# A three-layer expert FFN: its third layer as Strassen products over expert sums, with operands streamed from DRAM

## What is computed

```python
def _L0_ffn_ref(x, Wr, br, W1, b1, g1, be1, m1, v1, W2, b2, g2, be2, m2, v2, Wo, bo):
    feat = jnp.mean(x, axis=0)
    w = jax.nn.softmax(feat @ Wr + br, axis=-1)
    h = jnp.einsum('bfd,edh->bfeh', x, W1) + b1
    h = jax.nn.relu(_bn(h, g1, be1, m1, v1))
    h = jnp.einsum('bfeh,ehk->bfek', h, W2) + b2
    h = jax.nn.relu(_bn(h, g2, be2, m2, v2))
    y = jnp.einsum('bfeh,ehd->bfed', h, Wo) + bo
    return jnp.einsum('bfed,fe->bfd', y, w)

x = x + _L0_gnn_ref(_layernorm(x, axis=-1), adj, L0_gnn_W, L0_gnn_a)
x = x + _L0_ffn_ref(_layernorm(x, axis=-1), ...)
```

## Time and profile before

| | |
|---|---|
| median of 3 runs | 2948.12 us |
| the profiled execution: its own time, its span | 2946.45 us, 2944.7 us |
| mean granted TensorE clock | 0.994 |
| busy: PE, PEld | 2884.2 us (98%), 2423.9 us (82%) |
| busy: DVE, ACT, POOL | 1931.2 us (66%), 1697.9 us (58%), 730.2 us (25%) |
| DMA | 145.60 MB, mean 49 GB/s; 14 to 23 GB/s in the second stage |

### The profile page before, as it was taken

How to read it: one execution, slowest core, us unless ns; L and a number is a source line. 1 busy time by engine, 2 the same in 40 slices (tenths; PEclk the granted TensorE clock), 3 DMA queues, 4 the chain that set the end, 5 groups by cost and what they waited for, 6 DMA issues and landing times.

```text
span 2944.7 us, 42543 instructions
## 1 busy us (share of the span) xinstructions
PE 2884.2 (98%) x14806; PEld 2423.9 (82%) x14806; DVE 1931.2 (66%) x2843; ACT 1697.9 (58%) x2620; POOL 730.2 (25%) x894
## 2 busy tenths in 40 slices
PE   7999999998999999999999999999999999999998
PEld 7989898998888888888888888888888888888887
DVE  7999999996555555655556565556555565655554
ACT  7889888987444545444444445454544444454544
POOL 5888888887100000000000000000000000000000
PEclk9999999999999999999999999999999999999999
DMA  4444444443100000000000000000000000000000
GB/s 153 150 155 155 150 156 152 156 141 111 57 15 14 21 21 14 14 14 14 14 14 14 14 14 14 14 14 14 23 20 14 14 14 14 14 14 14 14 15 15
DMA packets 86037, 145.60 MB, mean 49 GB/s; under 512 B 7744, under 2 KB 63464, under 8 KB 86000
## 3 DMA queue, kind: packets, MB, share of 16 engines
q1 hardware_dynamic: 86000, 145.13, 14.7%
HBM read 111.52 MB, written 33.59 MB: 49 GB/s over the span
## 4 chain that ended last, share of the span: by engine, by line
PE 75%; DVE 0%; ACT 0%; issue 0%
PE z_ps L54 16%; PE z_ps L52 16%; PE z_ps L53 16%; PE y_ps L54 8%; PE y_ps L53 8%; PE y_ps L52 8%; PE turn_ps L931 1%; PE turn_ps L941 1%; PE y_ps L1016 0%; PE turn_ps L965 0%; PE y_ps L965 0%; PE z_ps L1009 0%; PE y_ps L1009 0%; ACT h L1048 0%; DVE h L1140 0%; DVE h_lo L1146 0%
## 5 line engine op out<-in xcount | busy, mean ns | idle before, releaser
L1048 ACT ACTIVATE h<-z_ps,bn_shift,bn_scale 128x512 f32<-128x512 f32 x1024 | 741.8, 775 | 1077.5 <-PE z_ps L54 1075.9
L1127 DVE TENSOR_TENSOR h_lo<-h,h_hi 128x1024 fp32r<-128x1024 f32 x256 | 321.6, 1256 | 762.5 <-ACT h_hi L1065 762.5
L86 POOL TENSOR_TENSOR ffn_vareps<-ffn_mv,ln_eps 128x4 f32<-128x4 f32 x32 | 6.4, 201 | 1880.0 <-DVE ffn_mv L80 1880.0
L52 PE MATMUL z_ps<-h_hi,w_hi 128*128 128x512 f32 x1024 | 410.3, 401 | 0.0
L54 PE MATMUL y_ps<-h_hi,wo_lo 128*128 128x512 f32 x1024 | 406.8, 397 | 0.0
L1140 DVE TENSOR_TENSOR h<-h,w_bc 128x1024 f32<-128x1024 f32 x256 | 313.8, 1226 | 140.9 <-ACT h L1048 137.0
L54 PE MATMUL z_ps<-h_hi,w_lo 128*128 128x512 f32 x1024 | 405.8, 396 | 0.0
L52 PE MATMUL z_ps<-xT_hi,w_hi 128*128 128x512 f32 x1024 | 405.2, 396 | 0.0
L53 PE MATMUL z_ps<-xT_lo,w_hi 128*128 128x512 f32 x1024 | 405.1, 396 | 0.0
L54 PE MATMUL z_ps<-xT_hi,w_lo 128*128 128x512 f32 x1024 | 405.0, 396 | 0.0
L53 PE MATMUL z_ps<-h_lo,w_hi 128*128 128x512 f32 x1024 | 405.0, 395 | 0.0
(11 more groups left out here) (128 smaller groups left out, 4876.6 us busy)
## 6 DMA issues: line engine op xcount, KB each, us to landing
adj_sb<-in_adj SPq DMA_DIRECT2D x128, 512.0 KB, 3.4
x_sb<-in_x SPq DMA_DIRECT2D x64, 256.0 KB, 2.8
x_scratch<-x_sb SPq DMA_DIRECT2D x128, 128.0 KB, 1.8
ffn_x<-x_scratch SPq DMA_DIRECT2D x32, 512.0 KB, 3.3
out<-ffn_x SPq DMA_DIRECT2D x32, 512.0 KB, 2.9
w_stage<-in_L_ffn_W SPq DMA_DIRECT2D x16, 256.0 KB, 4.0
w_bc<-w_scratch SPq DMA_DIRECT2D x8, 512.0 KB, 7.3
w_bc<-in_L_ffn_Wo SPq DMA_DIRECT2D x4, 512.0 KB, 5.9
```

What stands on the lines that cost most here:

```text
L52: pe.matmul(out, w_hi, x_hi, start=first, stop=False)
L86: pool.tensor_tensor(self.vareps[:, :], self.mv[:, :, 1], self.ln_eps[:, :], ALU.add) \
L1048: return act.activation(dst[:, m, :], src[:, m, :], ACT.Relu, bias=bn_shift[layer][:, col], scale=bn_scale[layer][:, col])
L1127: dve.tensor_tensor(h1_lo[i][:, :, :], h1[:, :, :], bits(h1_hi[i][:, :, :]), ALU.subtract) \
```

## The change

It touches `ffn_block` alone, in four ways.

First, layer three is a 2 x 2 block product, (2 x 128 outputs) x (2 x 128 inputs) on (2 x 256 nodes), done with Strassen's seven products in Winograd's form instead of eight. Each product has 256 columns and three split terms, 21 matmuls for a step. The seven products add up over the 8 experts in seven half banks (`m_ps`, 4 banks), and are combined once a tile.

Second, both sides of the products need sums. For the activations VectorE forms four differences from the gated h2 in each step (T1 and T3 in one instruction, then T2, then T4, each from the one before); h2's upper parts, now 7 x 256 = 1792 columns, are rounded by ScalarE in two copies, the lower ones subtracted by VectorE in two pieces. For Wo, GpSimd, ScalarE and VectorE form seven operands for each expert during the first tile and SyncE stores them to DRAM (`wo_dram`); from the second tile on they are loaded back step by step into two buffers (896 KB each), and a gate row too (256 KB, `load_gate`). The seven products of a tile are copied out by ScalarE and combined by seven adds on GpSimd (`combine`); for the last tile VectorE does this.

Third, `m_ps` needs four banks and `turn_ps` gets one, so layers one and two share three: `z1_bank, z2_bank = (0, 1), (2, 0)`. Bank 0 is used by both, and each half of a layer has its own semaphore count. Layer one now runs four steps ahead. TensorE's slot is layer two, transposes, layer three, layer one; the transposes come in groups of four in four slots.

Fourth, `residual` writes to buffers of its own (`res`), so x is loaded earlier, and xT is double buffered.

The core of the diff ("..." for what is left out):

```diff
+    Z1, Z2, Y = 4, 2, 1
+    PRODUCTS = ((P1, A11, B11), (P2, A12, B21), (P5, S1, T1), (P7, S3, T3), (P6, S2, T2), (P3, S4, B22), (P4, A22, T4))
...
-        z1_ps, z2_ps, y_ps, turn_ps = ps("z1_ps"), ps("z2_ps"), ps("y_ps"), ps("turn_ps")
+        z_ps, m_ps, turn_ps = ps("z_ps", 3), ps("m_ps", 4), ps("turn_ps", 1)
+        z1_bank, z2_bank = (0, 1), (2, 0)
...
+            def combine(n):
+                done = (n - 1) * COMBINES
+                pool.wait_ge(S["prod_ready"], n)
+                wait(pool, S["out_psum"], 2 * (n - 1))
+                def put(dst, left, right, op):
+                    pool.tensor_tensor(dst, left, right, op).then_inc(S["comb_ready"], 1)
+                put(prod[:, P6, :], prod[:, P1, :], prod[:, P6, :], ALU.add)
+                put(yT_sb[:, 0, HALF:], prod[:, P1, :], prod[:, P2, :], ALU.add)
+                pool.wait_ge(S["comb_ready"], done + 1)
+                put(prod[:, P7, :], prod[:, P7, :], prod[:, P6, :], ALU.add)
+                put(yT_sb[:, 0, :HALF], prod[:, P5, :], prod[:, P6, :], ALU.add)
...
+            def y_layer(e, w, x_hi, x_lo):
+                for q, a, t in PRODUCTS:
+                    w_hi, w_lo, x = w[:, 0, a - 1, :], w[:, 1, a - 1, :], t - 1
+                    begins = e == 0 and q in (P1, P2, P5, P4)
+                    pe.matmul(m_at(q), w_hi, x_hi[:, x, :], start=begins, stop=False, skip_group_check=True)
+                    pe.matmul(m_at(q), w_hi, x_lo[:, x, :], start=False, stop=False, skip_group_check=True)
+                    done = pe.matmul(m_at(q), w_lo, x_hi[:, x, :], start=False, stop=e == E - 1, skip_group_check=True)
...
             def slot(b, u, last):                      # TensorE
-                ok, c, e, n = step_at(b, u, 3, last)
+                ok, e, n = step_at(b, u, Z2, last)
                 if ok:
+                    i = u % 2
+                    pe.wait_ge(S["h1_lo_ready"], n)
+                    wait(pe, S["relu2_ready"], 2 * (n - 1) - 1)
+                    z_layer(1, e, 0, h1_hi[i], h1_lo[i])
+                    if step_at(b, u, Z2 + 1, last)[0]:
+                        pe.wait_ge(S["h1_ready"], 2 * n + 1)
+                    else:
+                        pe.wait_ge(S["relu2_ready"], 2 * (n - 1))
+                    z_layer(1, e, 1, h1_hi[i], h1_lo[i])
...
             def slot(b, u, last):                      # VectorE
...
+                    dve.tensor_tensor(h2[:, T1:T1 + 2, :], h2[:, B12, :].unsqueeze(1).to_broadcast([P, 2, HALF]),
+                                      h2[:, B11:B11 + 2, :], ALU.subtract).then_inc(S["t13_ready"], 1)
+                    dve.wait_ge(S["t13_ready"], n)
+                    dve.tensor_tensor(h2[:, T2, :], h2[:, B22, :], h2[:, T1, :], ALU.subtract) \
+                        .then_inc(S["t2_ready"], 1)
+                    dve.wait_ge(S["t2_ready"], n)
+                    dve.tensor_tensor(h2[:, T4, :], h2[:, T2, :], h2[:, B21, :], ALU.subtract) \
+                        .then_inc(S["t4_ready"], 1)
```

More of the change, by code:

```diff
@@ L882, in _ @@
+            for e in range(2):
+                load_sums(e)
+            sp.dma_start(x1_sb[1][:, :, :], x1_dram[1, 0]).then_inc(x1_in[1], DMA)
             sp.wait_ge(S["wT_ready"], 1)
@@ L895, in _ @@
-            for c in range(CH):
-                sp.wait_ge(stored[c], DMA * B)
+            for t in range(2):
+                load_gate(t)
+            for u in range(-Z1, 0):
+                slot(0, u, False)
+            for u in range(US):
+                slot(0, u, False)
+            with sp.Fori(1, B - 1) as b:
+                for u in range(US):
+                    slot(b, u, False)
+            for u in range(US):
+                slot(B - 1, u, True)
+            for h in (1, 0):
+                rows = slice(h * CT // 2, (h + 1) * CT // 2)
+                sp.wait_ge(S["out_ready"], 2 * B * CH - h)
+                sp.dma_start(out[B - 1].rearrange("(c s p) d -> c p s d", c=CH, p=P)[CH - 1][:, rows, :],
+                             res[CH - 1][:, rows, :]).then_inc(stored[CH - 1], DMA)
@@ new lines, in slot @@
+            def slot(b, u, last):
+                ok, c, n = next_tile(b, u, last)
+                if ok and u % E == 0:
+                    norm.deviation(pool, n)
+                if ok and u % E == 2:
+                    t = u // E - 1
+                    residual(c, n, None if opens(b) and t < 0 else DMA * (b + (t // CH + 1)))
+                if opens(b) and u + Y + 3 < E:
+                    weight_sums(u + Y + 3)
+                if u % E == E - 2 and not (last and u // E == CH - 1):
+                    combine(b * CH + (u // E + 1))
@@ new lines, in transpose_y, with z_layer @@
+            def transpose_y(acc, half):
+                for s in range(CT // 2):
+                    for d in range(KB):
+                        at = (half * CT // 2 + s) * P
+                        last = pe.transpose(acc[:, s * D + d * P:s * D + (d + 1) * P], yT_sb[:, d, at:at + P],
+                                            ident[:, :])
+                last.then_inc(S["out_psum"], 1)
+            def z_layer(layer, e, m, x_hi, x_lo):
+                acc = z_ps[:, (z1_bank, z2_bank)[layer][m], :]
+                for k in range(KB):
+                    at = slice(k * D + m * P, k * D + (m + 1) * P)
+                    done = split_matmul(pe, acc, w12_hi[:, layer, e, at], w12_lo[:, layer, e, at], x_hi[:, k, :],
+                                        x_lo[:, k, :], k == 0, k == KB - 1)
+                done.then_inc(S[("z1_ready", "z2_ready")[layer]], 1)
@@ L1109, in _ @@
+            for u in range(US):
+                slot(0, u, False)
+            with act.Fori(1, B - 1) as b:
+                for u in range(US):
+                    slot(b, u, False)
             for u in range(US):
```

536 lines of the change are left out of this document (313 added, 223 removed).

## The result

| | before | after |
|---|---|---|
| median | 2947.93 us | 3077.91 us (3075.92 to 3082.05, 4 runs) |
| ratio, 95% interval | | 1.0442 [1.0424, 1.046] |
| the profiled execution's own time, span | 2946.45, 2944.7 us | 3075.92, 3073.8 us |
| mean granted TensorE clock | 0.994 | 0.979 |

The account below looks back on a forecast made before the run. TensorE alone was taken to bound the second stage before the change. TensorE work -69, stops +140, first tile 8, opening 0, tail 2 gave +81 on 2946.5, itself 1.7 below the median: 3028 us, range 2912 to 3085.

Parts of the forecast that it names:

- TensorE's saving: Second stage: third layer as 21 matmuls of 256 columns, TensorE work per tile 66.8 instead of 68.97 us, 2.15 less.
- The loop of ScalarE and VectorE: Each second-stage step: the two engines take turns in a closed loop of 7.89 us, against TensorE's 8.11.
- Place one: The combination: product copies and GpSimd's adds beside VectorE make the loop late; TensorE stops 2.3 us a tile.
- The lock: VectorE and GpSimd share a port pair, held exclusively per instruction; without it the combination's stop would be some 0.3 us.
- Place two: The residual: GpSimd's 1024-column add, 2.41 us, holds up VectorE's gate product; TensorE stops some 1.1 us a tile.
- Place three: The x transposes: their second half waits for the single turn bank to be emptied, 0.8 us a tile.
- Streams at nothing: Loads of some 0.9 MB per 8 us step were taken to cost no time.
- Rival D: Stops of over 2 us at the combination drop TensorE's clock: +74 us, 3100 us, chance 0.11.
- Rivals B: The lock hardly bites, GpSimd's adds fall into VectorE's idle time: 2920 us, chance 0.18.
- C: All stops hide and TensorE alone decides: 2883 us, chance 0.05.
- E: Saving and stops cancel: 2942 to 2954 us, chance 0.06.
- the opening and tail: Ends of the kernel: opening taken as 0, between -5 and +5 us; tail +1 to +3, taken as 2.

Follow-up runs that it names:

- e4: e1 with VectorE's four Strassen differences also cut to 8 columns from the second sample on: 3009.90 us, ratio 1.0212.
- e14: e12 with the y transposes moved behind the third layer of their step and VectorE's out add behind the normalisation: 2914.81 us, ratio 0.9888.
- e1: Kernel after with GpSimd's seven combination adds cut from 256 to 8 columns from the second tile on: 3024.46 us, ratio 1.0191.
- e12: Kernel after with TensorE's loop written out, x halves split earlier, first-layer ReLU between the h2 copies, GpSimd's fourth add held until T4 is done: 2968.22 us.
- e3: Kernel before with each third-layer matmul of 512 columns cut into two of 256: 2986.22 us, ratio 1.0126.
- e8: Kernel after with TensorE's loop over the 14 middle samples written out: 3047.31 us, ratio 1.034.
- e11: e3 with TensorE's loop written out: 2961.76 us, ratio 1.0048.
- e9: e8 with the x halves split at the ends of steps 2 and 3 instead of inside steps 3 and 4: 3023.46 us, ratio 1.0258.

## Why the prediction was right in sign and 50 us short

- TensorE's saving, 2.15 us a tile: right to the digit. The tiles of e4 (without the jump) and e14, where little is late, take 67.0 to 67.9 against the 66.8 worked out.
- The loop of ScalarE and VectorE as what bounds the stage: right, and its terms too. Differences of 0.69, 0.42 and 0.43 us were estimated from neighbours at 0.69, 0.43 and 0.43.
- Place one: 2.10 us against 2.3. The lock was shown by e1 (adds short) and by e12 (adds moved in time): both take the stretching away. The Trainium skill's rule ("SBUF — State Buffer", SBUF: two separate sides) of an exclusive lock held for the whole instruction agrees in the alternation, but not quite in the whole instruction: VectorE's four were held up 0.41 to 0.57 us each, while an add alone takes 0.74, so a part of each ran side by side. The forecast's 0.45 to 0.6 came from rows and fits.
- Place two: 0.46 instead of 1.1, and not in all tiles. The step that failed is where the residual begins. It now has to wait for the store out of its own buffer to land (30 of 32 times), so it starts at 1292.87, 10.6 us after normalising ended at 1282.30, and hits a single difference instead of the gate product. VectorE's timeline there:

```profile
1293.35 2.50 DVE L1331 TENSOR_TENSOR h_sums<-h_sums 128x256 f32<-128x256 f32 x1
```

And GpSimd's:

```profile
1292.87 2.70 POOL L968 TENSOR_TENSOR ffn_res<-ffn_x,node_table 128x1024 f32<-128x1024 f32 x1 [14.86 <-DMA out<-ffn_res]
```

- Place three: 1.33 (0.38 in some tiles) instead of 0.8. In sum the three were 106 us, forecast 130.
- Streams at nothing: TensorE waited on no DMA, as the earlier trace rows suggested; 896 KB landed in 6.3 us. Their effect came by another way, in the length of the code stops (4.9 us with them, 2.7 without).
- The term that was missing: code, 27 us, forecast nothing. The forecast priced matmuls by their distance only, not by their number, and the kernel before could not show the price: its 36 matmuls per step brought 20 packets and no stop. e3 shows it at 48 matmuls, and e8 and e11 that writing the loop out ends it, worth 31 and 24 us (part of the 31 is clock).
- The term given to a rival: clock. Rival D had 0.11 and 74 us, one drop behind every stop of place one. It was more than half of that, 43 us, since 15 of 27 stops dropped it and the five long code stops all did. Half of rival D should have stood in the sum, as the bracket between 2.0 us (clock up) and 5.2 us (clock down) of the earlier trace rows offered no reason for the lower end.
- Rivals B, C and E are out: the adds stretch VectorE in every tile.

The two missing terms, 70 us, less the 24 by which the stops were overrated, and 8 more for the opening and tail give 54, against the 50. (The forecast's own sum, 2946.5 + 81 + 1.7, is 3029, not 3028.) That 3078 still lies 7 us inside the range of 2912 to 3085 is luck as far as code goes: no rival and no bound had a price for it.

Left open: why a pass of the loop fetches its code again or not (5 to 13 of 13, with the same matmuls and only the timing changed), why it then fetches nine packets for a body of six, and what decides the clock after a 2.1 us stop.

## What to carry to other kernels

A loop between two engines that fits TensorE's step with 0.2 us to spare has no room for anything that comes once a tile; look first for an instruction that a neighbour's wait holds up without needing it (here one ReLU, 62 us) and only then at durations. When GpSimd works beside VectorE, its adds are paid on VectorE; place them by a semaphore where VectorE's result is not awaited, and give their consumer a layer's time of cover: either alone gained nothing. Count a loop's instructions as well as their time. A pass of 608 matmuls was never fetched again here (before), one of 752 at 5 to 13 of 13 jumps (after and its variants), one of 800 at all 14 (e3); it shows as "issue" behind the branch and as packets on the instruction queue.

## What the runs showed of the hardware that was not expected

- Behind a loop's back branch TensorE stopped 1.3 to 1.9 us with quiet queues (e3, 14 of 14 jumps), and beside 145 GB/s of streams 0.7 to 1.0 and then 4.3 to 4.9 us (after, 5 of 13). Nine packets of 16.4 KB go with each such jump. The same code written straight on fetched 108 packets (e8) and did not stop.
- A stop of about 2.1 us was followed by the half clock in 15 of 27 cases (after), 11 of 32 (e8) and 23 of 31 (e9); the matmuls then start 0.43 and 0.21 apart instead of 0.23 and 0.12. None of the 30 waits below 1 us and of the 25 between 1.3 and 1.8 us was (after). In e3 none of 13 stops between 1.3 and 1.8 us was.
- GpSimd's two-input add of 256 columns takes 0.74 us alone and 1.46 in the median where it alternates with VectorE; a VectorE difference of 256 columns takes 0.42 alone and 0.85 there.
